# Three layers in one stream: a V projection, a layer norm and some copies moved later or earlier around the attention loop

## The reference

```python
x = x + 0.5 * ffn(layernorm(x), w1, b1, w2, b2)      # 256 -> 1024, exact gelu, -> 256
x = x + attn(layernorm(x), w_qkv, w_out, b_out)
x = x + 0.5 * ffn(layernorm(x), w1, b1, w2, b2)

def attn(x, w_qkv, w_out, b_out):                    # 16 heads of 64
    q, k, v = split(x @ w_qkv); q = q * 64 ** -0.5
    sim = q @ k.T - abs(j - i) * slope[head]         # masked where j > i
    return (softmax(sim) @ v) @ w_out + b_out
```

## Time and profile before

| | |
|---|---|
| median of 3 runs | 2344.89 us |
| profiled execution, whole | 2344.32 us |
| its span, first to last instruction | 2342.2 us |
| PE busy | 2191.1 us (94%) |
| DVE, ACT, POOL busy | 1552.3, 1208.7, 1052.2 us |
| mean granted TensorE clock | 0.978 |
| chain that ended last | PE 54%, DVE 22%, POOL 9%, ACT 6%, SP's queue 5% |
| load of one sequence's x (512 KB), issue to landing | 3.9 us |

### The profile page before, as it was taken

How to read it: one execution, slowest core, us unless ns; L and a number is a source line. 1 busy time by engine, 2 the same in 40 slices (tenths; PEclk the granted TensorE clock), 3 DMA queues, 4 the chain that set the end, 5 groups by cost and what they waited for, 6 DMA issues and landing times.

```text
span 2342.2 us, 41791 instructions
## 1 busy us (share of the span) xinstructions
PE 2191.1 (94%) x14720; PEld 1776.6 (76%) x14720; DVE 1552.3 (66%) x4070; ACT 1208.7 (52%) x3032; POOL 1052.2 (45%) x1770
## 2 busy tenths in 40 slices
PE   6899999999999999999999999999999999999987
PEld 5587787877878778787777878778787787877856
DVE  5675757667667676776757676576666767767563
ACT  4645636455363654736456364554636547364552
POOL 1543626436263453625537164362634536255260
PEclk9999999999999999999999999999999999999998
DMA  3332404224051340514314042240513405143150
GB/s 122 106 85 58 129 14 133 67 70 129 5 146 50 86 113 24 145 32 109 91 52 126 22 131 68 69 130 6 147 48 87 113 26 140 34 108 91 42 144 14
DMA packets 109936, 193.90 MB, mean 83 GB/s; under 512 B 34464, under 2 KB 53152, under 8 KB 109728
## 3 DMA queue, kind: packets, MB, share of 16 engines
q1 hardware_dynamic: 89248, 138.77, 21.1%
q0 software_dynamic: 20480, 52.47, 9.2%
HBM read 14.95 MB, written 8.39 MB: 10 GB/s over the span
## 4 chain that ended last, share of the span: by engine, by line
PE 54%; DVE 22%; POOL 9%; ACT 6%; SPq 5%; issue 3%; DMA 2%; POOLq 0%; DVEq 0%; ACTq 0%
PE ps L269 52%; DVE P L711 10%; POOL P L856 5%; DVE P L703 5%; SPq L219 5%; POOL PT L219 4%; ACT P L548 3%; DVE gl L636 3%; DVE gh L682 2%; DMA PT<-P 2%; PE ps L323 2%; ACT L548 1%; DVE xtl L636 1%; ACT v L515 0%; ACT qk L515 0%
## 5 line engine op out<-in xcount | busy, mean ns | idle before, releaser
L856 POOL TENSOR_SCALAR P<-P,rs 128x512 f32<-128x512 f32 (+3 forms) x1024 | 535.0, 539 | 474.3 <-DVE rs L694 470.9
L548 ACT ACTIVATE P<-P,mx 128x512 f32<-128x512 f32 (+3 forms) x1024 | 563.0, 552 | 239.5 <-DVE mx L703 238.9
L219 POOL DMA_DIRECT2D PT<-P x640 | 323.9, 511 | 350.9 <-DVE P L711 334.4
L711 DVE STREAM_TRANSPOSE P<-P 128x1792 f32<-128x1792 f32 (+1 forms) x256 | 385.0, 1504 | 64.2 <-POOL P L856 64.1
L269 PE MATMUL ps<-PT,v 128*64 128x256 f32 (+1 forms) x3072 | 323.4, 362 | 62.9 <-DMA PT<-P 60.4
L269 PE MATMUL ps<-qk 64*128 64x512 f32 (+3 forms) x2048 | 323.8, 446 | 36.5 <-DVE x L665 27.1
L269 PEld LDWEIGHTS ps<-PT,v 128*64 128x64 f32 x3072 | 222.4, 142 | 159.3 <-issue 81.3
L269 PE MATMUL ps<-w2h,gh 128*128 128x256 f32 x1024 | 302.3, 295 | 16.4 <-DVE gl L636 9.9
L269 PE MATMUL ps<-w2l,gh 128*128 128x256 f32 x1024 | 295.0, 288 | 0.0
L269 PE MATMUL ps<-w2h,gl 128*128 128x256 f32 x1024 | 294.4, 288 | 0.0
L269 PEld LDWEIGHTS ps<-qk 64*128 64x128 f32 x2048 | 171.8, 188 | 157.5 <-issue 76.9
(11 more groups left out here) (74 smaller groups left out, 4413.2 us busy)
## 6 DMA issues: line engine op xcount, KB each, us to landing
PT<-P SPq DMA_DIRECT2D x1408, 80.0 KB, 2.5
PT<-P POOLq DMA_DIRECT2D x640, 80.0 KB, 2.6
x<-in_L_attn_x SPq DMA_DIRECT2D x16, 512.0 KB, 3.9
out_y<-x SPq DMA_DIRECT2D x16, 512.0 KB, 2.9
raw<-in_L_ffn_w SPq DMA_DIRECT2D x2, 512.0 KB, 5.9
raw<-in_L_ffn_w SPq DMA_DIRECT2D x1, 1024.0 KB, 8.8
rawq<-in_L_attn_w_qkv SPq DMA_DIRECT2D x1, 1024.0 KB, 7.3
rawk<-in_L_attn_w_qkv SPq DMA_DIRECT2D x1, 1024.0 KB, 9.4
```

Of the source, the lines that this page charges most:

```text
L219: e.dma_start(PT[c % 2][32 * m:32 * m + 32, g, :], P[c % 3][32 * g:32 * g + 32, m, :]).then_inc(landed[c % 3].sem, 16)
L548: e.activation(p, p, ACT.Exp, bias=mx[:, r, i:i + 1], scale=-1.0, accum_out=sm[:, r, i:i + 1]).then_inc(s_ex.sem, 1)
L711: e.transpose(p, p).then_inc(s_tr.sem, 1)
L856: e.tensor_scalar(p, p, rs[:, 2 * (c % 2) + h, i:i + 1], 1.0, ALU.mult, ALU.mult).then_inc(s_nz.sem, 1)
```

## The change

It moves work in the hand-written lists; nothing is computed otherwise.

1. `v_tiles`: the last v tile, ("v", 3, 1), goes from pair 6 to pair 7.
2. PE: the two transposes of the next sequence's first layer norm, `ln_transpose(1, b+1, ..)`, go from the end of pair 6 (ahead of `scores(b, 7)`) to behind that v tile in pair 7, directly ahead of `up(1, b+1, 0)`.
3. ACT: `ln_hi(1, b+1, ..)` goes from the head of pair 7 to behind `exps(b, 7, 2)` and the copy of the v tile. DVE: `ln_lo(1, b+1, ..)` goes from the head of pair 7 to behind `turned(b, 6, 0)`.
4. `stats`/`variance` go from pair 4 to 5, `normal` from 5 to 6, `power` from 4 to 5; `store_y` and `load_x` from pair 0 to pairs 1 and 2.
5. ACT at the beginning of a sequence: the copies of k and q for pair 1 go behind `exps(b, 0, 3)`, and both copies for pair 2 go directly behind `exps(b, 1, 3)`.
6. Banks: `dn(2, b-1, 0)` takes bank 6 (before: 5), which the k tile of pair 1 held, and `scores(b, 1)` so no longer waits in bank 5 for `add3(b-1, 0)`. The second half of `ln_transpose(3, b, ..)` takes bank 0 (before: 6). Bank 0 is the first one that `scores(b+1, 0)`, next on PE, writes.

PE at the end of pair 6 and in pair 7, as it was. `ident,xn` are the transposes, `qk_77` the scores of pair 7, the first `xth,w1h` is `up(1, b+1, 0)`.

```diff
--- before.py
+++ after.py
@@ -105,7 +105,7 @@
     xts = {1: (xth, xtl), 2: (xth, xtl), 3: (x3h, x3l)}
 
     def v_tiles(c):
-        return {6: [("v", 3, 0), ("v", 3, 1)], 7: []}.get(c, [("v", c // 2, c % 2)] if c >= 2 else [])
+        return [("v", c // 2, c % 2)] if c >= 2 else []
 
     tiles = [("k", 0), ("q", 0), ("v", 0, 0), ("v", 0, 1)]
     FIRST = 4
@@ -255,9 +255,9 @@
             for b in B:
                 for c in range(NC):
                     spread(e, b, c, SPREAD_SP, s_pt)
-                    if c == 0 and b > 0:
+                    if c == 1 and b > 0:
                         store_y(b - 1)
-                    if c == 0 and b + 1 < NB:
+                    if c == 2 and b + 1 < NB:
                         load_x(b + 1)
             store_y(NB - 1)
             e.wait_ge(s_y.sem, s_y.at(NB - 1))
@@ -408,12 +408,11 @@
                 if b > 0:
                     among[0] = range(8)
                     up(2, b - 1, range(NM))
+                among[0] = (6, 7)
                 proj_tile(b, ("k", 1))
                 proj_tile(b, ("q", 1))
                 if b > 0:
-                    among[0] = (5,)
                     dn(2, b - 1, 0)
-                among[0] = (6, 7)
                 scores(b, 1)
                 if b > 0:
                     dn(2, b - 1, 1)
@@ -436,12 +435,10 @@
                         proj_tile(b, tile)
                     if more and c == NC - 1:
                         among[0] = (0, 1, 6, 7)
+                        ln_transpose(1, b + 1, 0)
+                        ln_transpose(1, b + 1, 1)
                         up(1, b + 1, range(3))
                     values(b, c - 2)
-                    if more and c == NC - 2:
-                        ln_transpose(1, b + 1, 0)
-                        among[0] = (5,)
-                        ln_transpose(1, b + 1, 1)
                 if more:
                     among[0] = (2, 3, 4, 5)
                     up(1, b + 1, range(3, 6))
@@ -482,10 +479,8 @@
                 if b + 1 < NB:
                     for tile in tiles[:FIRST]:
                         proj_tile(b + 1, tile)
-                among[0] = (6, 7)
                 ln_transpose(3, b, 0)
                 ln_transpose(3, b, 1)
-                among[0] = range(8)
                 if b + 1 < NB:
                     scores(b + 1, 0)
             up(2, NB - 1, range(NM))
@@ -554,20 +549,7 @@
 
             def attention(b):
                 more = b + 1 < NB
-                proj_copy(b, ("k", 1))
-                proj_copy(b, ("q", 1))
-                for i in QORDER:
-                    exps(b, 0, i)
-                exps(b, 1, 3)
-                proj_copy(b, ("k", 2))
-                exps(b, 1, 2)
-                exps(b, 1, 0)
-                proj_copy(b, ("q", 2))
-                exps(b, 1, 1)
-                for c in range(2, NC):
-                    if more and c == NC - 1:
-                        ln_hi(1, b + 1, 0)
-                        ln_hi(1, b + 1, 1)
+                for c in range(NC):
                     if c >= 3:
                         out_copy(b, c - 3)
                     exps(b, c, 3)
@@ -575,11 +557,12 @@
                         proj_copy(b, ("k", c + 1))
                         proj_copy(b, ("q", c + 1))
                     exps(b, c, 2)
-                    for tile in v_tiles(c)[:1]:
+                    for tile in v_tiles(c):
                         proj_copy(b, tile)
+                    if more and c == NC - 1:
+                        ln_hi(1, b + 1, 0)
+                        ln_hi(1, b + 1, 1)
                     exps(b, c, 0)
-                    for tile in v_tiles(c)[1:]:
-                        proj_copy(b, tile)
                     exps(b, c, 1)
                 if more:
                     gelu(1, b + 1, range(2))
@@ -739,23 +722,23 @@
                 more = b + 1 < NB
                 begin(b)
                 for c in range(2, NC):
-                    if more and c == NC - 1:
-                        ln_lo(1, b + 1, 0)
-                        ln_lo(1, b + 1, 1)
                     biased(b, c, 3)
                     inverse(b, c - 1, 0)
                     turned(b, c - 1, 1)
                     biased(b, c, 2)
                     turned(b, c - 1, 0)
+                    if more and c == NC - 1:
+                        ln_lo(1, b + 1, 0)
+                        ln_lo(1, b + 1, 1)
                     biased(b, c, 0)
                     biased(b, c, 1)
                     inverse(b, c, 1)
-                    if more and c == 4:
+                    if more and c == 5:
                         e.wait_ge(s_x.sem, s_x.at(b + 1))
                         for t in range(NT):
                             stats(1, b + 1, t)
                         variance(1, b + 1)
-                    if more and c == 5:
+                    if more and c == 6:
                         for t in range(NT):
                             normal(1, b + 1, t)
                 inverse(b, NC - 1, 0)
@@ -864,7 +847,7 @@
                         for h in range(2):
                             normalise(b, c, h, i)
                     if b + 1 < NB:
-                        if c == 4:
+                        if c == 5:
                             power(1, b + 1)
                         if c == NC - 1:
                             bias(1, b + 1)
```

## The result

The changed kernel took 2376.69 us (median of 4 runs, 2376.22 to 2377.54), the kernel before 2345.02 on the same chip: ratio 1.0135, interval 1.0117 to 1.0152, so 31.7 us slower. The forecast was 2376. The profiled execution is none of the four: it took 2378.08 us, with a span of 2375.9 us (before 2342.2) and a mean granted clock of 0.971 (before 0.978).

A forecast was written before the change was run, and what follows sets the result against it. PE, busy 94% of the span, was taken to bound the kernel through four waiting places. 15 x (1.4 + 1.7 - 0.2 - 0.4) = 37.5, less 5.8, is +31.7 on 2344.3: 2376 us, range 2353 to 2400.

The forecast's parts named there:

- `up` later, from scores 2 on: End of a sequence: `up(1, b+1, 0)` starts 5.6 us later because `ln_lo` stands behind `turned(b, 6, 0)`.
- waits that vanish behind it: From `up` through `dn(1, b+1, 0)`: 4.2 us of PE's waits for `values(b, 6)` and gelu splits vanish.
- clock: Behind the new wait ahead of `up`: lower clock costs +1.7 us per sequence, bounded by 0 and 2.2.
- projection to next scores (norm's bank): `scores(b+1, 0)` waits for both halves of the third layer norm because of bank 0: +1.2 us.
- beginning together: Beginning of a sequence: -0.2 us from ACT's line and -0.4 from slow clock stretches that go.
- once, beginning of the first sequence: First sequence only: exps start 4.9 us earlier and the q copy saves about 0.9 more, -5.8 us.
- Rival 1: Clock mostly stays at 2.4 GHz behind the longer wait, costing 0.3 for 1.7 us: 2355 us; chance 0.17.
- rival 2: The two new 1.4 us waits at a sequence's beginning cost clock too, 1.7 us more: 2401 us; chance 0.17.
- Faster or nothing: Two rivals: the beginning wins, 2316 us, chance 0.04; or remaining waits absorb the late `up`, 2342 to 2347, chance 0.04.
- The faster rival: Beginning loses its waits of 1.78, 0.89 and 0.25 us without new ones, -2.9 per sequence: 2316 us; chance 0.04.
- The 0.9 for the q copy of pair 2: First sequence: this copy now stands ahead of two pairs of exps, about -0.9 us more.
- DVE's last split was said to be 0.8 us late: Pair 7: DVE reaches the last gelu split 0.8 us later, while PE gets there 1.4 later.

The follow-up runs named there:

- fill_gap: The changed kernel with 16 more 128x512 matmuls on PE between the transposes and `up(1, b+1, 0)`; 2344.41 us, ratio to the kernel before 1.0011.
- act_only: The kernel before with only ACT's new order of exps and k and q copies, all banks as before; 2308.49 us, ratio 0.9856.
- begin_only: The kernel before with only ACT's new order of exps and copies and the two bank changes; 2327.62 us, ratio 0.9938.
- values_gap: The changed kernel with `values(b, 5)` ahead of the three `up` tiles, inside PE's wait; 2320.09 us, ratio to the kernel before 0.9893.
- best_end: Kernel before with ACT's new order, `dn(2, b-1, 0)` in bank 6, `add3(b-1, 1)` ahead of `turned(b, 0, 0)`, `values(b, 4)` behind `scores(b, 7)`; 2264.89 us, ratio 0.9661.
- best_bias: best_end with POOL's addition `bias(1, b+1)` moved behind its DMA issues of pair 7; 2293.26 us, ratio 0.9777.

## Why the prediction was right, point by point

| step, per sequence | predicted | measured | how |
|---|---|---|---|
| `up` later, from scores 2 on | +5.6 | +5.19 | 51.46 to 56.65 |
| waits that vanish behind it | -4.2 | -4.18 | 34.62 to 30.44 in fill_gap |
| clock | +1.7 | +2.12 | 32.56 - 30.44 |
| **end together** | +3.1 | +3.13 | |
| projection to next scores (norm's bank) | +1.2 | +1.32 | 19.49 to 20.81 |
| scores to scores 2 | -1.8 | -1.74 | 36.82 to 35.08 |
| **beginning together** | -0.6 | -0.42 | |
| **period** | +2.5 | +2.71 | 142.39 to 145.10 |
| once, beginning of the first sequence | -5.8 | -6.9 | scores to scores 2, 22.13 to 15.23 |

- **The end.** The mechanism held link by link, and the wait came out at 4.74 us in the sequence shown (3.80 to 5.29 over the 15), where 4.7 to 5.4 were forecast. Two sizes were off and cancelled: `up` is 0.4 less late, and the clock costs 0.4 more.
- **The clock.** This is the term that was mis-sized. I bounded it by 2.2 us from one row behind a wait of 4.40, and single sequences go up to 2.85. `up` is dense work, and it loses what falls into the slow stretch: its first three tiles took 5.77 and 6.95 us in the two sequences shown, in place of 4.31. "Only a part falls in the slow stretch" argued the wrong way. Rival 1, a cheap clock (0.3), is refuted: no sequence lies under 1.45.
- **The beginning.** The 1.72 and 1.38 us waits are there in all 15 sequences, forecast at 1.4 each. Behind neither did the clock fall: from the scores to scores 2 it takes 35.07 to 35.09 us in every one of them. Before, there were two levels, 36.62 without a slow stretch and about 36.95 with one (37.33 once, behind a wait of 2.15). That refutes rival 2. It also sizes the half-clock stretches that went: 0.2 in the mean, where I had 0.4. Without them the beginning gives 36.62 to 35.08 plus 1.32, which is -0.22, for a forecast of -0.2.
- **Faster or nothing.** The faster rival needed the k copy ahead of `dn(2, b-1, 0)`; it isn't (1.38 us). Nothing between `up` and the end of the sequence swallowed the delay.
- **The first sequence.** Of the 6.9 us, 4.9 are ACT's order (22.13 to 17.26 in act_only), as forecast. The 0.9 for the q copy of pair 2 did not show. The other 2.0 (17.26 to 15.24 in begin_only) are a term that the prediction left out: in this sequence the k and q tiles of pair 1 had banks 4 and 5, where PE waited for DVE to read the scores of pair 0, and edit 6 gives them banks 6 and 7. The wait in the kernel before, which the changed kernel doesn't have:

```profile
59.15 0.50 PE L269 MATMUL ps<-xth,wqh 128*128 128x512 f32 x1 [1.93 <-DVE mx L703]
```

- **A claim that was wrong and did no harm.** DVE's last split was said to be 0.8 us late. In values_gap it ends 73.6 us behind the scores of pair 2 and before 74.2 (means of 14), so it is not late at all.
- **The sum.** scores(1, 0) starts 2.3 us earlier (184.30 to 182.01: the 6.9, less 4.9 for the first end and the norm's bank, and 0.2 of the start), 14 periods give 14 x 2.71 = +37.9, and the last beginning -1.9 (from the last scores(b, 0) to the end, 164.4 to 162.5 us); together +33.7, the difference of the two spans. The medians differ by 31.7, the forecast was +31.7; that the two agree to a tenth is luck.

What stays open: why two neighbouring sequences of the changed kernel differ in how much of `up` falls into the slow stretch.

## What to carry to other kernels

Work on the critical engine that fills the time while others prepare its next operand must stay between the two; moving it ahead turned a hidden 1.9 us split, reached through three engines, into a 4.7 us wait. When two edits come together, time each by itself: here ACT's order alone was 1.4% faster, and one bank number (+1.3 us per sequence) and the order at the end (+3.1) hid it. A transfer wait is better removed by letting the work that feeds the transfer start earlier, as best_end does, than by delaying everything. And several short waits in a row can cost clock like one long one: best_bias lost more by that than by the waits themselves.

## What the runs showed of the hardware

- PE standing idle for 3.8 to 5.3 us cost 1.45 to 2.85 us more behind it, at a granted clock of 0.50 to 0.73 over the next 5.8 us; 3.9 us of useless matmuls in the same wait kept it at 1.00 and made the whole kernel some 30 us faster.
- The length of a single wait does not decide alone whether the clock falls. In the changed kernel waits of 1.38 and 1.72 us were never followed by a lower clock (15 each); in the kernel before, those of 1.78 in `scores(b, 1)` were in 8 of 15 sequences and those of about 2.2 ahead of `values(b, 6)` in 7 of 15, among them. But in best_bias three waits of 0.66, 0.45 and 0.45 us within 3 us, with a fourth just begun, were followed by 3.4 us at 0.51.
- DVE's cast of 128x512 took 0.38 us alone, 2.13 and 2.24 beside POOL's addition of 128x1024 (2.34 and 2.37 us), and 1.12 where it began 1.57 us into it; DVE's subtraction went from 0.69 to 3.61 us beside the same addition. Its record begins 0.64 us ahead of POOL's there and ends 0.55 behind it, so by these records even the one that began first was held up; starts on POOL are rough, and I leave the cause open.
